# Pooling's sums of weights by one product for a batch's four tiles, and the edge type table computed at the end of attention

## What is computed

```python
# one attention layer
msg = jnp.einsum('ehg,egd->ehd', attn, V[tgt]).reshape(-1, HID)
msg = msg + Ee[et]
proj = msg @ Wo.T + bo
return jax.ops.segment_sum(proj, src, num_segments=n_nodes)
...
# pooling
w = jnp.exp(-jax.nn.relu(score / 20.0))
pooled = jax.vmap(lambda wi, fi: seg(wi[:, None] * fi))(w, dst_f)
row_sum = jax.vmap(lambda wi: seg(wi))(w)
out = pooled / row_sum[:, :, None]
```

## Time and profile before

| what | value |
|---|---|
| median of three runs | 5239.12 us (5237.07 to 5248.7) |
| the profiled execution | 5233.94 us, its span 5232.0 us |
| PE busy | 3759.6 us (72%), 36105 matmul instructions |
| DVE busy | 2729.3 us (52%) |
| POOL busy | 2424.9 us (46%) |
| pooling's gathers (L1904) | 412, busy 411.1 us |
| pooling's feature sums (L2033) | 3328 instructions, busy 298.9 us |
| pooling's sums of weights (L2035) | 1664 instructions, busy 220.8 us |

### The profile page before, as it was taken

How to read it: one execution, slowest core, us unless ns; L and a number is a source line. 1 busy time by engine, 2 the same in 40 slices (tenths; PEclk the granted TensorE clock), 3 DMA queues, 4 the chain that set the end, 5 groups by cost and what they waited for, 6 DMA issues and landing times. The chain is left out here.

```text
span 5232.0 us, 112793 instructions
## 1 busy us (share of the span) xinstructions
PE 3759.6 (72%) x36105; PEld 2965.2 (57%) x36105; DVE 2729.3 (52%) x8902; ACT 1515.5 (29%) x6308; POOL 2424.9 (46%) x2373
## 2 busy tenths in 40 slices
PE   4666554888888788888887888888856455555677
PEld 3444332677777557777764777776645344444566
DVE  7666665556556545565554566565424233333423
ACT  1222220433334133333323333332222111121122
POOL 2666565455555145555523555553035444444201
PEclk9985556888788888888888788787867555555579
DMA  1110004455555145555523455553047222222100
GB/s 61 41 41 17 1 1 135 127 143 144 141 140 144 45 125 143 141 143 142 144 59 114 129 144 143 145 143 95 31 140 139 67 65 65 65 65 65 32 26 20
DMA packets 209041, 493.57 MB, mean 94 GB/s; under 512 B 73145, under 2 KB 97301, under 8 KB 207880
## 3 DMA queue, kind: packets, MB, share of 16 engines
q0 software_dynamic: 149120, 429.71, 29.7%
q1 hardware_dynamic: 59799, 62.33, 3.9%
HBM read 430.59 MB, written 62.94 MB: 94 GB/s over the span
## 5 line engine op out<-in xcount | busy, mean ns | idle before, releaser
L1144 POOL DMA_INDIRECT kv<-kv_table,ae_idx x1200 | 1232.4, 1027 | 1017.5 <-ACT ae_idx L1177 702.8
L1287 PE MATMUL sc_ps<-ae_q,ae_kT 64*128 64x64 f32 x9984 | 802.0, 312 | 97.3 <-issue 95.8
L1287 PEld LDWEIGHTS sc_ps<-ae_q,ae_kT 64*128 64x128 f32 x9984 | 741.6, 222 | 211.1 <-issue 202.2
L1221 DVE TENSOR_REDUCE ae_own<-sc_ps 128x64 f32<-128x1024 f32 x312 | 382.1, 1225 | 734.8 <-PE sc_ps L1287 502.2
L1300 PE MATMUL out_ps<-hid,kv 128*64 128x64 f32 x9984 | 529.3, 264 | 114.4 <-issue 90.2
L1904 POOL DMA_INDIRECT kv<-feature_table,pe_idx x412 | 411.1, 998 | 423.8 <-ACT pe_idx L1938 313.3
L741 POOL DMA_INDIRECT edge_records<-rec_c,idx x416 | 422.7, 1016 | 352.9 <-ACT rec_c L501 224.2
L1300 PEld LDWEIGHTS out_ps<-hid,kv 128*64 128x64 f32 x9984 | 449.7, 173 | 211.8 <-issue 189.6
L1154 ACT ACTIVATE ae_kT<-kT_ps 128x512 f32<-128x512 f32 x624 | 365.1, 595 | 665.3 <-PE kT_ps L1269 487.3
L1205 DVE TENSOR_TENSOR totals<-totals,out_ps 128x32 f32 x2496 | 447.1, 179 | 209.9 <-DVE totals L1205 4.1
L2033 PE MATMUL pe_out<-pe_wgt,kv 128*64 128x16 f32 x3328 | 298.9, 264 | 309.4 <-issue 224.4
(11 more groups left out here) (448 smaller groups left out, 5736.8 us busy)
## 6 DMA issues: line engine op xcount, KB each, us to landing
kv<-kv_table,ae_idx POOLq DMA_INDIRECT x1200
et_w<-in_EW SPq DMA_DIRECT2D x56, 192.5 KB
expert_in<-kv SPq DMA_DIRECT2D x14, 512.0 KB
et_xs<-expert_in SPq DMA_DIRECT2D x56, 128.0 KB, 3.8
expert_out<-et_o POOLq DMA_DIRECT2D x56, 128.0 KB, 3.6
edge_records<-rec_c,idx POOLq DMA_INDIRECT x416
kv<-feature_table,pe_idx POOLq DMA_INDIRECT x412
nodes_placed<-kv SPq DMA_DIRECT2D x12, 512.0 KB
```

Of the source, the lines that this page charges most:

```text
L1144: pool.indirect_dma_start(kv[:, k, u, :], None, kv_d, bass.IndirectOffsetOnAxis(ap=idx[:, k, u:u + 1], axis=0), bounds_check=last_row, oob ...
L1221: v.tensor_reduce(own[:, j, :, :].rearrange("p g x -> p (g x)"), sc_ps[:, j, :, :, :].rearrange("p e i (x w) -> p (e i x) w", w=W), axis=A ...
L1287: last = pe.matmul(sc_ps[:, k % 2, e, i, u * HW:(u + 1) * HW], kT[rows, u, i, :], q[rows, k % FEW, u, :, :].rearrange("p h w -> p (h w)"), ...
```

## The change

In pooling the two products with `ones_f` move out of the loop over the four tiles: each now runs once per batch over all four tiles' weights, 128 moving columns, after the sixteen feature products.

The table is computed at the end of the attention block: PE waits until the weights have landed, forms the four products into a part of `kT_ps` and says `ew_ready`; DVE adds the bias after its last adds and writes the table into a free piece of `qT`. The node update reads it from there and starts with the node products.

```diff
@@ update_parts
-            flat[0:DH, at[3]:at[3] + 3 * H].rearrange("p (h n) -> p h n", h=H), qT[0:3, 1, :], y[:, 0], y[:, 1])
+            flat[0:DH, at[3]:at[3] + 3 * H].rearrange("p (h n) -> p h n", h=H), flat[0:3, at[3] + D:at[3] + 2 * D],
+            qT[0:3, 1, :], y[:, 0], y[:, 1])
@@ attention_edges, vector, after the last adds
+                _, _, _, bo, _, ew, _, _, _ = update_parts(qT)
+                v.wait_ge(m.ew_ready, 1)
+                v.tensor_tensor(ew, kT_ps[0:3, 0, :, :].rearrange("p i n -> p (i n)"), bo, ALU.add)
@@ attention_edges, tensor, after the last sums
+                wo, _, _, _, ee, _, _, _, _ = update_parts(qT)
+                pe.wait_ge(m.weights_loaded, 96)
+                for h in range(H):
+                    last = pe.matmul(kT_ps[0:3, 0, :, :].rearrange("p i n -> p (i n)"), ee[:, h, :], wo[0:DH, h, :], start=h == 0, stop=h == H - 1)
+                last.then_inc(m.ew_ready, 1)
@@ node_update, tensor
-                for h in range(H):
-                    last = pe.matmul(ew_ps[0:3, 0:D], ee[:, h, :], wo[0:DH, h, :], start=h == 0, stop=h == H - 1)
-                last.then_inc(m.ew_ready, 1)
-                pe.wait_ge(m.ew_done, 1)
...
-                        pe.matmul(o, types[:, nodes], ew[:, :], start=False, stop=True).then_inc(m.used, 1)
+                        pe.matmul(o, types[:, nodes], ew, start=False, stop=True).then_inc(m.used, 1)
@@ node_update, vector
-                v.wait_ge(m.ew_ready, 1)
-                v.tensor_tensor(ew[:, :], ew_ps[0:3, 0:D], bo[:, :], ALU.add).then_inc(m.ew_done, 1)
@@ pooling_edges, tensor, sums
-                        for e in range(2):
-                            last = pe.matmul(out_ps[e * DH:(e + 1) * DH, k % 2, u * HW + 2 * W:(u + 1) * HW], ones_f[:, :],
-                                             wgt[:, k % 2, u, :, :].rearrange("p (a e) w -> p e a w", e=2)[:, e, :, :], start=True, stop=True)
+                    for e in range(2):
+                        last = pe.matmul(out_ps[e * DH:(e + 1) * DH, k % 2, 0:BT * HW].rearrange("p (u x) -> p u x", x=HW)[:, :, 2 * W:HW], ones_f[:, :],
+                                         wgt[:, k % 2, :, :, :].rearrange("p u (a e) w -> p e (u a) w", e=2)[:, e, :, :], start=True, stop=True)
```

More of the change, by code:

```diff
@@ L1119, in attention_edges @@
                    "scores_ready", "own_ready", "top_ready", "low_ready", "exp_ready", "z_ready", "rz_ready",
-                   "att_ready", "weights_ready", "sums_ready", "added", "weights_loaded", ends=(loaded,)) as (block, m):
+                   "att_ready", "weights_ready", "sums_ready", "added", "weights_loaded", "ew_ready", ends=(loaded,)) as (block, m):
             @block.sync
@@ L1124, in _ @@
                 one = bass.ds(layer, 1)
-                wo, gam, bet, bo, ee, types, _, _ = update_parts(qT)
+                wo, gam, bet, bo, ee, _, types, _, _ = update_parts(qT)
                 sp.wait_ge(m.q_ready, BATCHES * ROW)
@@ L1316, in _ @@
                     sums(b, None, b % SETS)
+                wo, _, _, _, ee, _, _, _, _ = update_parts(qT)
[3 more added lines that the diff above has]
+                last.then_inc(m.ew_ready, 1)
 def node_update(nc, t, sb, pb, g):
     hid, eps, totals = g["hid"], g["eps"], g["totals"]
-    wo, gam, bet, bo, ee, types, y, yn = update_parts(g["qT"])
+    wo, gam, bet, _, _, ew, types, y, yn = update_parts(g["qT"])
     with ExitStack() as st:
@@ L1325, in s @@
             return sb("nu_" + name, shape, dt, st)
-        ew = s("ew", (3, D))
         stats, mv, std, rstd = ln_buffers(s)
-        ew_ps, prod = pb(st, "ew_ps", (P, 512)), pb(st, "nu_prod", (P, 3, 512))
-        with phase(nc, "nu", "ew_ready", "ew_done", "hid_back", "used", "added+dve", "turn",
+        prod = pb(st, "nu_prod", (P, 3, 512))
+        with phase(nc, "nu", "hid_back", "used", "added+dve", "turn",
                    "ln_step", "std_ready", "scaled", "shifted", "done+act") as (block, m):
```

## The result

| | before | changed |
|---|---|---|
| median, ten runs each on one chip | 5240.77 us | 5220.55 us |
| ratio, 95% interval | | 0.996 [0.9941, 0.998] |
| the profiled execution: span | 5232.0 us | 5225.0 us |
| first to last gather of pooling (411 starts apart) | 827.4 us | 817.3 us |
| last sums to first node product, each layer | 10.91 us | 7.22 us |

The changed kernel is 0.4% faster, some 20 us where 5.5 were forecast. The spans of the two profiled executions differ by only 7.0 us, because the changed one lost time again in stages whose code is the same: from its first to its last product of scores (`sc_ps`) the third attention loop took 762.5 us against 755.1, and the products that make pooling's features (`fe_prod`, the stage ahead of pooling) took 59.7 against 53.2.

What follows compares the result with a forecast made beforehand. No engine is full; pooling is bound by a 16.4 us round of eight gathers with PE's sums beside the chain, the node update by the small table. 5239.1 - 0 - 5.5 = 5233.6 us, range 5219 to 5247.

Steps and rivals of the forecast that it cites:

- within 0.2%: Whole kernel: the time changes by less than about 10.5 us, which a measurement can't tell from no change; chance 0.67.
- rival (a): Node update: the clock follows the work, or rises sooner because PE stays busy; -11 to -19 us, 5220 to 5228; chance 0.21.
- 2.67 us of slack: Pooling round: 1.29 us before VectorE takes the second scores plus 1.38 us before the fifth gather, hiding added PE work.
- slack of 1.29 us: Pooling round: time from PE's end of the second scores at 4412.31 to VectorE taking them at 4413.60.
- Part 1's work on PE: Pooling's sums of weights: merged products take 0.88 us a batch as before, bounds -0.43 to +0.89 us.
- rival (b): Pooling: three batches a round through a third index, 7.2 us a batch instead of 8.2, about -100 us, 5140; chance 0.05.
- Part 1's worth: Pooling: the change in PE's sums hides in slack, so 0 on the round and 0 us over 52 rounds.
- Part 2's shift: Node update: node products start 4.07 - 0.41 = 3.66 us earlier a layer, 11.0 us for three.
- Part 2's discount: Node update: the clock rises at the same moment as before, so 3.66 us a layer is worth 1.83, 5.5 in all.
- (c): Pooling: the wide products run badly and use up both slacks; +44 us, 5283; chance 0.08 with any other slowing in pooling.
- (e): End of attention: the table's products wait for something and aren't hidden, so the cost only moves; 5239; chance 0.07.
- (d): Node update: the clock rises 7 us later in each layer; 10.2 lost against 5.5 gained, +5 us, 5244; chance 0.07.

Runs made afterwards that it cites:

- the long rows: Changed kernel with the feature table's rows padded from 260 to 512 numbers (1040 to 2048 bytes): 5291.34 us, ratio 0.9968 to the kernel before.
- the first comparison: The whole change against the kernel before, ten runs each on one chip: 5220.55 us against 5240.77 us, ratio 0.996.
- the last experiment: Changed kernel with added identity products keeping PE busy at the end of each attention layer: 5276.22 us, ratio 0.996; on another chip 5282.0 us, 0.9936.
- the three comparisons: The whole change against the kernel before, on three chips: medians 5220.55, 5289.61 and 5216.41 us.

## Why the prediction was right or wrong

The forecast was 5233.6 us, 0.1% below before; what came is 20 us, 0.4%. The range 5219 to 5247 holds the changed kernel's median; the likeliest case, "within 0.2%", did not come. It stood at 0.67, the side that came at 0.25. That the range holds is in part luck. Its lower end was drawn for a clock that rises sooner, rival (a)'s second half, which did not come; the room was filled by pooling, for which the sum had 0, and the median lies 1.6 us from the edge. By the prediction's own sign of being wrong, "a change in pooling of more than a few us", its half on pooling was wrong.

- **What bounds pooling.** The rounds of eight gathers and the crawl were read rightly, and both are still there, though the crawl goes with the gathers and not with their packets, as the long rows show. The step that failed is "PE is in it only with the scores' completion. Its sums are beside it." PE works in order, so the sums ahead of the scores are in that completion. Doubling them showed it: +1.1 us a round where 2.67 us of slack had been counted. The slack of 1.29 us was measured between a recorded end of the scores and VectorE's start, at a place of the round where no gather runs; the place that decides is the other one, at the start of the burst.
- **Part 1's work on PE.** Bounds -0.43 to +0.89 us a batch, 0 taken; it is 0.61 - 0.88 = -0.27. The two halves of the columns do stream beside each other for part of the time, as the lower bound had it. The rule of the Trainium skill cited at rival (b) ("TensorE: Matmul & The Clock Gate", Packing small matmuls), that column tiles run concurrently, would give 0.45 by the prediction's estimate; the trace bears it out by some two thirds.
- **Part 1's worth.** Term 0, measured by the traces -5.1 us on the slow first chip, -10.1 in the first comparison, and -10.9 and -8.0 on the fast chip. This is the largest miss of the sum. Some 0.1 us comes in each round, for a reason that the runs don't show; where the gain is larger, 3 to 5 us come in the first burst, which the prediction did not look at at all.
- **Part 2's shift.** 3.66 us a layer forecast, 3.69 measured; the cover (VectorE's last adds), the visible bias add and the landed weights were as read.
- **Part 2's discount.** "If the rise comes at the same moment as before" was taken, for 5.5 us; the rise comes at its own distance behind the phase's first product, so all 11.1 us stay. That is the first half of rival (a). Its second half, a rise that comes sooner, did not come with the change; it takes more work on PE ahead of the phase, as the last experiment showed.
- **The sum.** By the traces -11.1 and -5.1 to -10.9 make -16 to -22 us; the medians of the three comparisons differ by 20.2, 14.3 and 19.2 us (ratios 0.9960, 0.9957, 0.9964).
- **Rivals.** (b) was rightly priced as just too late, but for a wrong reason: in the changed kernel the scores of every round behind the first burst start before the crawl, 2.4 to 2.5 us behind the burst's first gather, and it doesn't help. A start is not enough; behind the first burst the third index came once in each of three traces, where the gathers paused. (c) and (e) are out by the rows above; (d) is out by the means of the node products.

## What to carry to other kernels

Where an engine's completions are held back while gathers run, ask of every instruction on it whether it stands ahead of the one that others wait for when the gathers begin; the slack is to be read there, and an end recorded by the profiler is not yet a signal received. Where a low clock follows a phase's own start, as here, it moves with the phase, and work moved out of the phase is worth its full time. And a first, longer burst ahead of a loop deserves its own look: on one chip it held about half of part 1's gain, on two others nothing.

## What the runs showed of the hardware

- Some us into a burst of gathers PE slows to one small matmul every 0.7 to 1.4 us (8 in 6.4 us), and in a regular round scores started 9 us before are seen by VectorE only 2.4 to 2.7 us behind the start of the last gather. Rows of 1040, 1088 and 2048 bytes behave alike, though the packets of the longest run on for 0.6 us past VectorE's restart. In a first burst of 20 gathers on one chip the scores came through 16.3 us behind their start, while gathers still ran. The cause is open.
- The Trainium skill ("SBUF — State Buffer", Who interferes with whom) says that DMA never contends with a compute engine. These traces show PE held back in step with the gathers; whether that is contention in the page's sense they can't tell.
- Two f32 products of 128 columns into the two halves of the array hold PE for 0.61 us at a granted clock of 0.50, where eight of 32 columns held it for 0.88.
- Twenty f32 instructions on the identity behind the table and thirty-two ahead of the last sums (52 in all, in place of idle time) kept the granted clock at 1.00 across a gap of 1.70 us, in all six layers traced.
